# A ViT tower on one core: set-up transfers in order of need, constant products on TensorE ahead of the first inputs, and image 0's projections in front of its row maxima

## The reference

```python
out = jnp.einsum('bnd,ed->bne', patches, W) + b + pos          # h, (32, 1024, 64)
q = src @ Wq.T + bq;  k = src @ Wk.T + bk;  v = src @ Wv.T + bv
scores = jnp.einsum('bid,bjd->bij', q, k) * scale               # masked where q[..., 0] or k[..., 0] is 0
prob = jax.nn.softmax(scores, axis=-1)
out = jnp.einsum('bij,bjd->bid', prob, v);  return out @ Wo.T + bo
...
h = _layernorm(h + _L0_attn_ref(h, ...), axis=-1)
h = _layernorm(h + _L0_ffn_ref(h, ...), axis=-1)                # 8 experts, top 1, capacity per expert
```

## Time and profile before

| | |
|---|---|
| median of 3 runs | 1049.55 us |
| the profiled execution's own time | 1052.52 us |
| its span in the trace | 1050.7 us |
| TensorE busy | 945.6 us (90%) |
| VectorE busy | 854.0 us (81%) |
| ScalarE busy | 708.1 us (67%) |
| GpSimd busy | 586.2 us (56%) |
| mean granted clock of TensorE | 0.953 |

### The profile page before, as it was taken

The page is one execution under the profiler, slowest core; times in us unless marked ns, Lnnn a source line. Parts: engine busy times, 40 slices in busy tenths (PEclk is TensorE's granted clock), DMA queues, the critical chain, the costliest instruction groups (busy, mean ns, idle before and its releaser), DMA issues.

```text
span 1050.7 us, 19710 instructions
## 1 busy us (share of the span) xinstructions
PE 945.6 (90%) x6046; PEld 530.5 (50%) x6046; DVE 854.0 (81%) x1771; ACT 708.1 (67%) x1254; POOL 586.2 (56%) x564
## 2 busy tenths in 40 slices
PE   4799999999999999999999999999999999846640
PEld 2355555555555555555555555555555555433320
DVE  3667788789898989999898989898999988675561
ACT  2365665777777777777777777777777766636650
POOL 0003333335666666666666666666666666776775
PEclk9699999999999999999999999999999999958775
DMA  3322223333434343343434333434333432235200
GB/s 96 80 64 68 59 60 100 99 92 88 117 83 119 96 106 93 98 107 103 110 95 109 105 103 84 118 89 113 102 99 91 108 96 71 87 86 175 63 20 11
DMA packets 72504, 96.25 MB, mean 92 GB/s; under 512 B 15923, under 2 KB 52230, under 8 KB 72398
## 3 DMA queue, kind: packets, MB, share of 16 engines
q1 hardware_dynamic: 55566, 77.87, 28.9%
q0 software_dynamic: 16832, 17.11, 5.1%
HBM read 43.68 MB, written 18.11 MB: 59 GB/s over the span
## 4 chain that ended last, share of the span: by engine, by line
PE 51%; DVE 29%; issue 9%; ACT 8%; DMA 1%; POOL 1%; SPq 0%; POOLq 0%; ACTq 0%; DVEq 0%
PE p_u L601 14%; PE p_st L579 9%; DVE mx L1028 8%; PE p_misc L616 6%; PE p_misc L547 4%; PE p_misc L664 3%; ACT uu L807 3%; PE p_sm L561 3%; PE p_st L583 3%; DVE lo L1020 2%; DVE qk L1013 2%; PE p_misc L524 2%; PE p_sm L680 2%; ACT b_h L852 2%; PE p_misc L680 1%
## 5 line engine op out<-in xcount | busy, mean ns | idle before, releaser
L1399 POOL DMA_INDIRECT slots<-rows,idx x256 | 251.2, 981 | 275.5 <-issue 166.9
L1412 POOL DMA_INDIRECT out<-b_o,b_ix x270 | 294.7, 1091 | 86.7 <-issue 81.7
L1028 DVE TENSOR_REDUCE mx<-p_sm 128x1 f32<-128x1024 f32 x252 | 306.9, 1218 | 35.1 <-PE p_sm L563 33.7
L802 ACT ACTIVATE pT<-p_st 128x1024 f32<-128x1024 f32 x256 | 262.0, 1023 | 92.2 <-PE p_st L585 80.8
L601 PE MATMUL p_u<-pT,vv 128*64 128x512 f32 x1024 | 254.1, 607 | 0.0
L579 PE MATMUL p_st<-hi,hx 64*128 64x512 f32 x256 | 127.4, 498 | 6.2 <-ACT pT L802 4.4
L581 PE MATMUL p_st<-hx,hi 64*128 64x512 f32 x256 | 127.4, 498 | 0.0
L601 PEld LDWEIGHTS p_u<-pT,vv 128*64 128x64 f32 x1024 | 61.8, 136 | 106.2 <-issue 94.4
L579 PEld LDWEIGHTS p_st<-hi,hx 64*128 64x128 f32 x256 | 47.0, 184 | 128.5 <-issue 100.3
L561 PE MATMUL p_sm<-kh,hi 64*128 64x512 f32 x252 | 100.7, 399 | 5.1 <-DMA hx<-hi 3.5
L852 ACT ACTIVATE b_h<-p_misc,b_w 128x256 f32<-128x256 f32 x244 | 95.8, 476 | 13.1 <-PE p_misc L664 6.5
(11 more groups left out here) (189 smaller groups left out, 1818.7 us busy)
## 6 DMA issues: line engine op xcount, KB each, us to landing
b_w<-in_w SPq DMA_DIRECT2D x136, 193.5 KB
hx<-hi SPq DMA_DIRECT2D x64, 256.0 KB, 3.6
b_in<-slots SPq DMA_DIRECT2D x136, 66.0 KB
lx<-lo SPq DMA_DIRECT2D x32, 256.0 KB, 3.1
xt<-in_x SPq DMA_DIRECT2D x32, 196.0 KB
out<-b_o,b_ix POOLq DMA_INDIRECT x270
kh<-kh SPq DMA_DIRECT2D x32, 128.0 KB, 2.3
lx<-lo SPq DMA_DIRECT2D x32, 128.0 KB, 3.0
```

Source lines behind the costliest of these rows:

```text
L802: act.activation(pT[k % 4][:, :], flat(p_st), ACT.Exp).then_inc(exp_done, 1)
L1028: dve.tensor_reduce(mx[:, p, at:at + 1], flat(max_place(n, j)), AX.X, ALU.max).then_inc(max_done, 1)
L1399: pool.indirect_dma_start(slots, bass.IndirectOffsetOnAxis(ap=idx[:, p, j:j + 1], axis=0), rows[:, p, j, :], None, bounds_check=SLOTS - 1, ...
L1412: pool.indirect_dma_start(out_rows, bass.IndirectOffsetOnAxis(ap=b_ix[:, o, j:j + 1], axis=0), b_o[:, o, j, :], None, bounds_check=T - 1, ...
```

## The change

It has four parts.

1. **Transfers.** SyncE issues `c_deep` and `w_qk` first, then `posT` for image 0 alone, then `x` 0, `c_wide`, `posT` for images 1 and 2, `x` 1 and 2. The first two count on `deep_loaded`, the third on `pos_loaded`, the rest of the old four on `w_loaded` (`NW` = 2). The first of the two `hx` transfers of image 0 counts on a semaphore of its own, `spread_first`, which is all that the first row maxima wait for; `scores` of image 0 waits for the second.
2. **Order of the set-up.** `w_e` times `w_qk`, from which `w_qkx` comes, is the first product now; the products for `w_px` and `w_j` come after image 0's qk product (`projections`). VectorE's memset of `xt` is split, one third ahead of the set-up and two thirds within it. `key_steps(0)` stands in the set-up, ahead of the copy of `w_px`, and what needs `c_wide` comes last.
3. **Constant products.** `busy(n)` issues n products of `ones_r` (128 x 128, all ones) with itself into `p_misc`, which nothing reads: 14 ahead of the wait for `deep_loaded` and 12 behind the set-up's small products, ahead of image 0's qk product.
4. **Projections of image 0.** The first half runs ahead of image 1's qk product as before, the second half right behind it, into `p_st` instead of `p_misc`; it stood in the loop of the maxima at k = 6. The second pair of `max_scores` of image 0, which writes `p_st`, waits for `v_ready` 2, ScalarE's copy of that half. The wait for `kh_ready` 2 moves to image 2's qk product.

The diff, without the declarations of semaphores, ScalarE's start (it no longer waits for `w_loaded` or `setup_v`), the copies and memsets at the set-up's end, the loops' new conditions, the new place in `projected` (`p_u` for the first half of image 0, `p_st` for the second) and GpSimd's count on `const_set`:

```diff
--- before.py
+++ after.py
...
@@ -362,7 +365,7 @@
 
         def projected(n, r):
 
-            return p_u if n == 0 and r == 0 else p_misc
+            return (p_u, p_st)[r] if n == 0 else p_misc
 
         def after(eng, s, value):
 
@@ -386,10 +389,12 @@
         @block.sync
         def _(sp):
 
+            sp.dma_start(c_deep[:, :], deep).then_inc(deep_loaded, 16)
+            sp.dma_start(w_qk[:, :], wqk).then_inc(deep_loaded, 16)
+            sp.dma_start(xt[0:D, 0, :], posT).then_inc(pos_loaded, 16)
             sp.dma_start(xt[KA:KTOK, 0, :], x[0, :, :]).then_inc(x_loaded[0], 16)
-            for dst, src in ((c_deep[:, :], deep), (w_qk[:, :], wqk),
-                             (xt[0:D, :, :], posT.unsqueeze(1).broadcast_to([D, 3, S])), (c_wide[:, :], wide)):
-                sp.dma_start(dst, src).then_inc(w_loaded, 16)
+            sp.dma_start(c_wide[:, :], wide).then_inc(w_loaded, 16)
+            sp.dma_start(xt[0:D, 1:3, :], posT.unsqueeze(1).broadcast_to([D, 2, S])).then_inc(w_loaded, 16)
             for n in (1, 2):
                 sp.dma_start(xt[KA:KTOK, n, :], x[n, :, :]).then_inc(x_loaded[n], 16)
 
@@ -453,8 +458,9 @@
                 sp.wait_ge(hi_ready, n + 1)
                 if n >= 3:
                     sp.wait_ge(st_done, NT * (n - 2))
-                for dst, src in ((hx[t][D:P, :], hi[t][0:D, :]), (hx[t][0:D, :], hi[t][D:P, :])):
-                    sp.dma_start(dst.bitcast(F32), src.bitcast(F32)).then_inc(spread_hi[t], 16)
+                sp.dma_start(hx[t][D:P, :].bitcast(F32), hi[t][0:D, :].bitcast(F32))\
+                    .then_inc(spread_first if n == 0 else spread_hi[t], 16)
+                sp.dma_start(hx[t][0:D, :].bitcast(F32), hi[t][D:P, :].bitcast(F32)).then_inc(spread_hi[t], 16)
 
             def spread_low(n):
                 t = n % 3
@@ -493,27 +499,46 @@
         @block.tensor
         def _(pe):
 
-            pe.wait_ge(w_loaded, 16 * NW)
+            def busy(n):
+
+                for _ in range(n):
+                    pe.matmul(p_misc[:, 1, 0:P], ones_r[:, :], ones_r[:, :], start=True, stop=True)
+
+            pe.wait_ge(const_set, 1)
+            busy(14)
+            pe.wait_ge(deep_loaded, 32)
             pe.wait_ge(setup_v, 1)
-            pe.matmul(p_misc[0:D, 0, 0:D], w_v[:, :], w_oTp[:, :], start=True, stop=True)
-            pe.matmul(p_misc[0:D, 1, 0:E], c_centre[:, :], w_g[:, :], start=True, stop=True)
-            pe.matmul(p_sm[0:D, 0, 0:1], w_oTp[:, :], w_bv[:, :], start=True, stop=True)\
+            pe.matmul(p_u[0:KTOK, 0, 0:2 * D], w_e[:, :], w_qk[:, :], start=True, stop=True)\
                 .then_inc(setup_p, 1)
             pe.wait_ge(setup_v, 2)
-            pe.matmul(p_st[0:KA, 0, 0:CG], w_bl[:, :], w_cg[:, :], start=True, stop=True)
-            pe.matmul(p_st[:, 1, 0:CG], w_lj[:, :], w_cg[:, :], start=True, stop=True)\
+            pe.matmul(p_sm[0:D, 0, 0:D], w_v[:, :], w_oTp[:, :], start=True, stop=True)
+            pe.matmul(p_sm[0:D, 1, 0:E], c_centre[:, :], w_g[:, :], start=True, stop=True)
+            pe.matmul(p_st[0:D, 0, 0:1], w_oTp[:, :], w_bv[:, :], start=True, stop=True)\
                 .then_inc(setup_p, 1)
-            pe.matmul(p_u[0:KTOK, 0, 0:2 * D], w_e[:, :], w_qk[:, :], start=True, stop=True)
-            pe.wait_ge(setup_v, 3)
-            pe.matmul(p_u[0:KTOK, 1, 0:GP], w_e[:, :], w_all[:, :], start=True, stop=True)\
-                .then_inc(setup_p, 1)
-            pe.wait_ge(setup_v, 4)
+            busy(12)
+
+            def projections():
+                pe.wait_ge(setup_v, 4)
+                pe.matmul(p_st[0:KA, 0, 0:CG], w_bl[:, :], w_cg[:, :], start=True, stop=True)
+                pe.matmul(p_st[:, 1, 0:CG], w_lj[:, :], w_cg[:, :], start=True, stop=True)\
+                    .then_inc(setup_p, 1)
+                pe.wait_ge(setup_v, 5)
+                pe.matmul(p_u[0:KTOK, 1, 0:GP], w_e[:, :], w_all[:, :], start=True, stop=True)\
+                    .then_inc(setup_p, 1)
+                pe.wait_ge(setup_v, 6)
 
             def after_qk(n):
 
                 pe.wait_ge(kh_ready, n + 1)
 
             def qk_product(n, p):
+                if n == 0:
+                    pe.wait_ge(pos_loaded, 16)
+                    pe.wait_ge(setup_v, 3)
+                if n == 1:
+                    pe.wait_ge(w_loaded, 16 * NW)
+                if n == 2:
+                    after_qk(1)
                 pe.wait_ge(x_loaded[n % 3], 16 * (n // 3) + 16)
                 if isinstance(n, int) and n == 1:
                     after_qk(0)
@@ -536,9 +561,7 @@
                         pe.wait_ge(b_xT_ready, chunk_of(n - 1) + 1)
                     if chunk_of(n - 2) is not None:
                         pe.wait_ge(b_p_ready, chunk_of(n - 2) + 1)
-                elif n == 0:
-                    after_qk(1)
-                else:
+                elif n > 0:
                     pe.wait_ge(v_ready, 2 * n + 1)
                     if chunk_of(n - 1) is not None:
                         pe.wait_ge(b_relu, 2 * PAIRS * HB * (chunk_of(n - 1) + 1))
@@ -552,11 +575,16 @@
                 t = n % 3
                 if j == 0:
                     pe.wait_ge(spread_kh[n % 2], 16 * (n // 2) + 16)
-                    pe.wait_ge(spread_hi[t], 32 * (n // 3) + 32)
+                    if n == 0:
+                        pe.wait_ge(spread_first, 16)
+                    else:
+                        pe.wait_ge(spread_hi[t], 32 * (n // 3) + (16 if t == 0 else 32))
                     after(pe, shift_ready, n)
                     after(pe, pos_read, n - 2)
 
                 after(pe, max_done, j - 1 if n == 0 else NT * n + j)
+                if n == 0 and j == 1:
+                    pe.wait_ge(v_ready, 2)
 
                 pe.matmul(max_place(n, j)[:, 0, :], hi[t][0:D, j * P:(j + 1) * P], kh[n % 2][0:D, 0:HALF],
                           start=True, stop=True)
@@ -570,6 +598,8 @@
             def scores(n, k):
                 t = n % 3
                 if k == 0:
+                    if n == 0:
+                        pe.wait_ge(spread_hi[t], 16)
                     pe.wait_ge(spread_lo[t], 32 * (n // 3) + 32)
                     pe.wait_ge(shift_ready, n + 1)
                 after(pe, exp_done, NT * n + k)
@@ -706,9 +736,12 @@
                 if has(-2) and b < NB:
                     positions(b - 2)
                 if b == -1:
+                    projections()
                     project(0, q, 0, True)
                 if has(2):
                     qk_product(b + 2, par)
+                if b == -1:
+                    project(0, q, 1, True)
                 m, back = chunk_of(b), chunk_of(b - 1)
                 for k in range(NT):
                     if has(0):
...
@@ -891,8 +922,12 @@
                 par = c % 2
                 q = 1 - par
                 m, back, done = chunk_of(b), chunk_of(b - 1), chunk_of(b - 2)
+                if b == -1:
+                    v_copy(0, q, 0)
                 if has(2):
                     qk_copy(b + 2)
+                if b == -1:
+                    v_copy(0, q, 1)
                 for k in range(NT):
                     if k == KHK and has(2):
                         k_high(b + 2)
...
@@ -964,54 +999,56 @@
                 ins.then_inc(set_link, 1)
                 dve.wait_ge(set_link, links[0])
 
-            dve.memset(xt[D:KA, :, :], 1.0)
+            def key_steps(n):
+                dve.wait_ge(qk_ready, n + 1)
+                dve.tensor_tensor(qk[D:P, 0:S - P], qk[D:P, 0:S - P], flat(p_misc)[D:P, P:S], ALU.subtract)\
+                    .then_inc(dk_ready, 1)
+
+            dve.memset(ones_r[:, :].bitcast(F32), 1.0).then_inc(const_set, 1)
             dve.memset(w_all[:, :], 0.0)
             dve.memset(w_e[D:KA, :], 0.0).then_inc(set_link, 1)
             dve.wait_ge(set_link, 1)
             dve.memset(w_e[D:KA, D:KA], 1.0).then_inc(const_set, 1)
-            dve.wait_ge(const_set, 1)
-            dve.wait_ge(w_loaded, 16 * NW)
+            dve.memset(xt[D:KA, 0, :], 1.0)
+            dve.wait_ge(const_set, 2)
+            dve.wait_ge(deep_loaded, 32)
+            dve.tensor_copy(w_e[0:D, :], w_t[:, :]).then_inc(setup_v, 1)
             dve.tensor_scalar(w_oTp[:, :], w_oT[:, :], w_oT[:, D - 1:D], None, ALU.subtract)\
                 .then_inc(setup_v, 1)
-            dve.tensor_copy(w_e[0:D, :], w_t[:, :])
             dve.tensor_copy(w_all[:, GP - 2:GP - 1], w_qk[:, 0:1])
             dve.tensor_copy(w_all[:, GP - 1:GP], w_qk[:, D:D + 1])
-            dve.tensor_copy(w_j[:, GT - 1:GT], c_sum[:, :])
             dve.tensor_copy(w_cg[:, 0:D], c_centre[:, :])
-            dve.tensor_copy(w_lj[:, 0:D], c_id[0:D, 0:D])
-            link(dve.tensor_copy(w_lj[:, D:P], c_id[0:D, 0:D]))
+            dve.tensor_copy(w_lj[:, 0:D], w_bl[:, 0:D])
+            link(dve.tensor_copy(w_lj[:, D:P], w_bl[:, 0:D]))
             dve.wait_ge(setup_p, 1)
-            dve.tensor_copy(w_all[0:D, 0:D - 1], p_misc[0:D, 0, 0:D - 1])
```

(22 more changed lines are left out.)

20 lines of the change are left out of this document (8 added, 12 removed).

## The result

The changed kernel takes 1043.85 us (median of 6 runs, 1042.3 to 1045.91), the one before 1049.51 (6 runs, 1049.13 to 1050.97): 0.9938 of it, 95% interval 0.9926 to 0.995. That is 5.7 us faster where 10.6 were forecast, and just outside the widest range stated (to 1043.0). The six runs form two groups: 1042.3 to 1042.72 at a mean granted clock of 0.953 to 0.955, and 1044.97 to 1045.91 at 0.951. The profiled execution is of the first group: time 1042.3, span 1040.5. Against the profiled execution of before (span 1050.7) that is 10.2 us, close to the forecast by luck: about 2 of the 10.2 are a longer stretch at half clock in that one execution of before, as the experiments show.

The account below looks back on a forecast made before the run. The middle was taken as bound by TensorE (811.5 of 820 us busy), so savings in the start's chain of waits reach the end: 8.2 + 0.85 + 1.57 = 10.6 us off 1049.55 gives 1038.95, own range 1037.0 to 1041.2, 8-in-10 range 1035.8 to 1043.0.

Parts of the forecast that it names:

- rival 3: Something behind the first 40 us sets the pace and the gain is given back later: 1049.5 us, chance 5%.
- T: End of image 0's qk product in the start: forecast 9.6 against 17.84 us, 8.2 us saved.
- I take 0.15: Time in us of each 128 x 128 constant product in the start; the 12 were to take 1.8.
- I take 6: Time in us by which the first four transfers, x 0 the last, have landed, sooner than TensorE asks for them.
- range for T: From 8.2 (12 products at 0.105 and a fast qk product) to 10.9 us.
- So I take 2.4: Image 0's qk product takes 2.4 us, between 1.95 and 3.80, since TensorE's dense work has raised the clock.
- From T to the first maximum: Stretch from T to image 0's first row maximum: 8.75 us in place of 9.61, 0.85 saved.
- only at the upper clock: Condition that TensorE, ScalarE and VectorE work behind T fits under T + 8.75, the first maximum.
- Rival 1: TensorE stays at the lower level until the maxima: T 11.0, first maximum 22.4, time 1042.9 us, chance 17%.
- the differences do not scale with it: The profiled execution, 3 us above the median, was taken to leave the forecast savings unchanged.

Follow-up runs that it names:

- e5: Changed kernel with the second half of image 0's projections back in the loop of the maxima; 0.9897 of the kernel before.
- e3: Changed kernel without any of its 26 constant products; 0.9938 of the kernel before.
- e4: Changed kernel without the 12 constant products ahead of image 0's qk product, the 14 kept; 0.9953 of the kernel before.
- e9: Changed kernel without the 12 constant products, x 0 loaded as 48 rows and 1; 0.9921 or 0.9935 of before (the text does not clearly say which).
- e17: Changed kernel with its 14 and 12 narrow constant products replaced by 6 and 5 of 512 columns; 0.9883 of the kernel before.
- e18: Changed kernel with x 0 split, 6 and 2 wide constant products, 3 behind the last set-up product, maxima and first scores filled; 0.9883 of before.
- e8: Changed kernel run again unedited for another profile; second turn (turn product behind image 1's row maxima) 56.75 us; its own time is not singled out.
- before again: The kernel before, run again unedited for a second profile; 23.5 us between the turn products behind image 0's and image 1's maxima; own time not singled out.
- e6: Changed kernel plus 46 unread products: 8 narrow behind the last set-up product, 3 wide behind each maxima pair and image 0's first two scores; 0.9917 of before.

## Why the prediction came out as it did

**Right in mechanism: only the start is touched, and its gain is kept.** The middle is as before, and the nearly constant remainder of six traces shows it; rival 3 (given back later) falls. The 6.2 us at T come from parts 1 and 2 of the change, net of the 0.5 to 0.6 that the 12 products cost; the two were not taken out one by one. Part 4 is right to 0.01 us: 9.14 against 10.72 is 1.58 saved, 1.57 forecast, and `e5` gives it back. `w_e` is copied at 3.36 (3.5 forecast) and T to the last maximum holds no new wait; that for `v_ready` 2 costs nothing.

**The 12 constant products, mis-sized.** "I take 0.15" was 0.235 each, 2.82 in all: the qk product starts at 8.09, not 7.2. What they cost, 0.5 to 0.6, is smaller than the forecast's 1.2, because its landing time for `x` 0, "I take 6", was 7.4 in truth (`e3`, `e4`). The prediction took the 333 KB moved by 4.00 for the first three transfers complete; that does not follow, for other transfers were under way, and `x` 0, issued at 0.74 in before, takes 4.8 to 5.0 us from issue in `e3` and `e4`. So that `w_e` came on time (3.36) does not bear the reading out. The Trainium skill ("DMA: Bandwidth & Descriptors", "Why a DMA increments its semaphore by 16 and not by 1") says that a transfer goes to the largest number of engines, up to 16, that divides the outer dimension of both its sides; my estimate from that page is 7 engines for 49 rows and 16 for 48. The split agrees: 4.8 to 5.0 us become 3.83 in `e9`; the engines themselves were not counted. The range for T has a slip too: with the 12 at 0.105 and a fast qk product alone its own terms give 8.6, and 8.2 only if the two transfers also land at their lower bound.

**The clock, the step that failed.** "TensorE has worked almost without a gap for 5.5 us. So I take 2.4" for the first qk product: it took 3.2 to 3.75 in each trace with narrow products or none. I carried the rise before, 6 us into dense work, over to another kind of work: by then the kernel before had done qk records of 512 columns, the changed one only narrow products. Behind six wide ones in the place of the 14 the level was up by the set-up products (`e17`, `e18`), and in `e18`, after the shorter wait, in the qk product too, shown by one trace each. The Trainium skill ("TensorE: Matmul & The Clock Gate", Part 1) names sustained activity as what releases the clock; the narrow products, with no gap in the records, did not bring it about ahead of the qk product in any trace here. This step cost 1.1 of the 8.2 us at T, the start of the product 0.9.

**From T to the first maximum: 0.23 saved and not 0.85.** This is the same failed step a second time: the sum held "only at the upper clock", and after the wait from 12 to 14 the clock fell, so that the second qk product took 3.10 for 1.95, and the ScalarE copy and the subtraction behind it came last. `e9` shows how strong this is: 1.4 us sooner at T, nothing sooner at the first maximum. With the upper level held (`e18`) the stretch is 8.1 us and ends with the `hx` transfer, as the forecast's 8.75 does.

**Rival 1 got 17% and came up in one of after's four traces.** `e8` has first maximum 22.31 (22.4 forecast, partly by luck) and second turn 56.75. With the 986.8 behind it and 1.8 of time outside the span this gives 1045.3, the slower group, three of after's six runs; the profile's 53.74 gives 1042.3, the faster one. The rival's own time, 1042.9, was 2.4 lower; 1.7 of that is the second fall of the clock between the turns (25.2 and not 23.5), which it did not have. That the faster group lies at 1042.3 to 1042.72, near the rival's number, is chance. That the two groups are these two patterns is worked out from one trace each and the clock shares, not shown run by run.

**The accounting.** 10.6 forecast; 8.0 seen at the last maximum; half of the runs in the later group take off about 1.4, which leaves 6.6. Measured are 5.7. Of the rest I can say only this: before's second turn in its two traces is 62.2 or later, so 1050.8 or more, close to its median on chip 15 (1050.7), while the 1049.5 of the first runs would need 60.9. No trace shows that. About 1 us stays open.

**What I overlooked in the profile.** It was 3 us above the median and the prediction said that "the differences do not scale with it". They don't, but about 2 of the 3 us had a place: 25.4 between the turns where before again has 23.5, with a clock at 0.50 for longer (mean granted clock 0.82 and 0.89). The same work at the start has a price that differs by up to 2 us between executions of one kernel, more than the terms from T to the first maximum (0.85) and for the projections (1.57).

## What to carry to other kernels

Price TensorE's work at a kernel's start at the lower level, and give the clock a case of its own for every wait that the change makes or leaves there: an earlier product is worth nothing if those behind the next wait then run at half speed. Constant products ahead of the first inputs are worth trying in the width of the real ones and ending close to the landing of the operands, together with filled holes behind them. Here width alone and the earlier landing alone gave nothing at the second turn, filling alone 0.9 us or more, and the three together the earliest turn by 3 us, in one trace; the times are too coarse to confirm it. When a profile is slower than the median, find the stretch that holds the difference before you set another profile beside it.

## What the chip showed that I had not expected

- The granted clock column reads 1.00 in the first microseconds, though the 26 narrow products (0.235 each) and the qk product (3.54) are at the lower level. In `e8` it still reads 1.00 from 16 to 20, where the second qk product takes 3.52. Ahead of the first rise only durations tell the level.
- Constant products of 128 columns took 0.235 us each at the lower level (the loads of their weights cover 5.7 of the 6.1 us of all 26) and 0.14 at the upper (`e6`, eight in 1.10), where a 512-column one took 0.49 and 0.29.
- A wait of 1.46 us after the rise was followed by the lower level (`e17`), one of 1.04 us was not (`e18`); one trace each.
- On chips 8, 4 and 5 TensorE, VectorE and ScalarE stand still together, up to 6 us at a time, from about 100 us on. Between 60 and 960 us this makes 36 us in before again, 46 in `e9` and 40 in `e17`, and nothing in the profiles of before and after. VectorE's row maxima wait 197 us in before again for a signal that the profile calls remote. In the stretch 300 to 400 of before again TensorE is busy 80.52 of 100 us, and 99.11 in before; what it comes from was not studied:

```profile
300.00:400.00 100.00, 80.52 (x484) 44.84 (x480) 65.56 (x129) 55.28 (x96) 49.70 (x50) 0.91 0.29 76
```
